# Attention steps that convert expert weights: two experts in each of four early steps, none in the last four

## The chip, the cores and the metric

The kernel runs on one core of a Trainium2 chip. The metric is the device time of one execution in microseconds. Three runs of the kernel before took 386.76, 388.03 and 394.06 us; their median, 388.03 us, is the time before. The profile is of one further execution.

## The reference

Sixteen batch items of 128 rows by 256 columns pass through two stages, each added to its input.

```
x = x + xattn(layernorm(x), ctx)     # per item: theta, phi and g projections to 64 latents, scores, softmax,
                                     # p @ g, normalisation over the whole latent, relu, out projection, + ctx
x = x + moe(layernorm(x))            # 2048 tokens: router softmax, top 2 of 4 groups, top 4 of 16 experts,
                                     # silu(x W1) * (x W3) @ W2 per chosen expert, weighted; plus two shared experts
```

Every product on the expert side is done with 16-bit weights split into a high and a low half. The weights come from memory as 32-bit numbers, 18 sets of them (two shared experts and sixteen routed ones), and have to be converted into the two halves on the chip.

## The kernel before, in words

Attention is a software pipeline over the sixteen items. A step index s runs from 0 to 20; in step s each engine works on parts of several items, and a helper `tile(s, v, lag, part)` (line 326) calls the part for item s minus lag if that item exists. Steps 0 to 7 are written out, steps 8 to 15 are a hardware loop of four steps per pass, steps 16 to 20 are written out again. The order of the calls in each engine's `step` function is the order in which the engine runs them; no engine overtakes within its own list.

The weights ride along in the same steps. SP loads one set (608 KB) at a time into one of two staging buffers, `wst` (line 402); the load for set e waits until set e-2 has been fully converted (line 401, semaphore `wl_ready`). ACT makes the high half with a scaled copy (`weights_high`, line 466, lag 2, the instruction is line 469), which waits for its load; it stands behind `normalise` at the end of the step, and the exponentials of the next step follow it (line 485). DVE makes the low half (`weights_low`, line 1041, lag 3, the instruction is line 1044), which waits for the high half; it stands between the last instruction of the latent normalisation (`latent_out`, line 996) and the second layer norm (`normalise2`, line 1034). So with one set per step ACT converts set s-2 in steps 2 to 19, and DVE set s-3 in steps 3 to 20.

Other lines that the prediction touches: on TensorE the transposes of the softmax p (line 651, they wait for the exponentials), the transposes of the latent (line 676, they wait for DVE's `latent_out`), the product of p and g (`attend`, line 661) and the scores (line 642), in this order around a step's end; the router matmuls (line 698). On DVE the row maximum (line 945) that the exponentials wait for, and the low half of the relu (line 933). On POOL the reciprocal root, an epsilon addition and a power (`rstd`, lines 1440 and 1442), on which `latent_out` and `normalise2` wait; in the later steps POOL also issues the scatters of token rows (line 1460), and `rstd` stands between the second and the third scatter of its step.

After the attention come the units of the shared experts for the first twelve items, with the last four items' routing woven in on DVE, then 80 tiles of the routed experts, then the rest. TensorE waits for all 18 sets only before the routed experts.

Of the kernel before, what the change touches and what calls it, by code (L numbers as in the profile page):

```python
# [35 lines left out]
NU = NE + 2  # L36
# [33 lines left out]
def build(nc, x, ctx_in, params, halves, w_in, out):  # L70
# [4 lines left out]
    with ExitStack() as stack:  # L75
# [152 lines left out]
        def part(n, k):  # L228

            at = 2 * WU + (k * (B // CB) + n) * 2 * CB * T  # L230
            return w[:, at:at + 2 * CB * T].bitcast(F32)
# [94 lines left out]
        def tile(s, v, lag, part, count=B):  # L326

            if not isinstance(s, int) or 0 <= s - lag < count:
                part(s - lag, (v - lag) % 4)

        def group(s, v, lag, part):

            if (v - lag) % 4 == 0 and (not isinstance(s, int) or 0 <= s - lag < B - 4):
                part(s - lag)
# [127 lines left out]
        def _(act):  # L462
# [64 lines left out]
            def step(s, v):  # L527

                tile(s, v, 2, exps)
                tile(s, v, 5, copy_xT)  # L530
                tile(s, v, 1, theta_phi)
                tile(s, v, 2, copy_pT)
                tile(s, v, 3, relu)
                tile(s, v, 4, high)
                tile(s, v, 0, normalise)
                tile(s, v, 2, weights_high, count=NU)
                group(s, v, 8, route_exp)

            def gate(G, n, j, m):
# [20 lines left out]
            def between(stage, n):  # L560
                if stage == "R":
                    route_exp(B - Q)

            pipeline(act, step, units, T_LAG[0], between)

            flat = scatter_rows.rearrange("r c -> (r c)")
# [39 lines left out]
        def _(pe):  # L606
# [108 lines left out]
            def step(s, v):  # L715

                tile(s, v, 2, scores)
                tile(s, v, 4, project_out)
                tile(s, v, 3, mean_all)
                tile(s, v, 1, theta)  # L720
                tile(s, v, 5, transpose_rows)
                tile(s, v, 1, phi)
                group(s, v, 10, count)
                tile(s, v, 2, transpose_p)
                tile(s, v, 1, project_g)
                tile(s, v, 5, router)
                tile(s, v, 3, transpose_h)
                tile(s, v, 2, attend)
# [172 lines left out]
        def _(dve):  # L901
# [106 lines left out]
            def late(s, v, lag, part):  # L1008

                if not isinstance(s, int) or s >= FIRST:  # L1010
                    tile(s, v, lag, part)
# [178 lines left out]
            def step(s, v):  # L1190

                late(s, v, 5, low)
                tile(s, v, 3, attended)
                tile(s, v, 3, latent_stats)
                group(s, v, 10, chosen_diff)
                tile(s, v, 3, latent_aggr)
                group(s, v, 9, route_sum)
                tile(s, v, 3, latent_moments)
                group(s, v, 10, chosen)
                group(s, v, 9, route_recip)  # L1200
                tile(s, v, 2, row_max)
                group(s, v, 10, rank_scan)
                group(s, v, 9, route_score)
                tile(s, v, 4, residual)
                group(s, v, 10, rank_mask)
                group(s, v, 9, group_max)
                tile(s, v, 3, latent_all)
                tile(s, v, 2, values)
                group(s, v, 9, group_compare)
                tile(s, v, 3, latent_var)  # L1210
                tile(s, v, 4, stats2)
                group(s, v, 10, rank_one_hot)
                group(s, v, 10, slots)
                group(s, v, 9, group_equal)
                tile(s, v, 3, latent_centre)
                tile(s, v, 4, aggr2)
                group(s, v, 9, group_before)
                group(s, v, 10, slots_by_rank)
                group(s, v, 9, group_rank)
                tile(s, v, 3, latent_out)  # L1220
                group(s, v, 9, group_choose)
                tile(s, v, 3, weights_low, count=NU)
                group(s, v, 9, mask_mult)
                group(s, v, 10, token_weights)
                group(s, v, 10, destinations)
                group(s, v, 10, slots_sum)
                tile(s, v, 4, normalise2)
                late(s, v, 2, add_context)
                group(s, v, 9, mask_add)
                tile(s, v, 5, logits)  # L1230
                group(s, v, 10, slots_out)
                group(s, v, 9, top_values)
                tile(s, v, 2, recip)
                group(s, v, 9, top_four)
                tile(s, v, 3, relu_low)
                group(s, v, 8, route_max)
                group(s, v, 9, top_replace)
                group(s, v, 8, route_less_max)
# [122 lines left out]
            def last_units(n, first, last):  # L1361
                hidden(SH, n, n % 2, n % 2)
                hidden_low(SH, n, n % 2, SH["hlo_ready"], 1)

            pipeline(dve, step, first_units, D_LAG[0], lambda stage, n: stage in ("A", "R") and between(stage, n))

            def estep(s, step_v, r):
# [195 lines left out]
```

## Time and profile before

| what | value |
|---|---|
| runs, median (lowest to highest) | 388.03 us (386.76 to 394.06) |
| the profiled execution, its own time | 391.98 us |
| its span, first to last instruction | 390.0 us |
| TensorE busy, granted clock over the span | 331.2 us (85%), 0.838 |
| DVE, ACT, POOL busy | 259.5, 221.1, 189.7 us |
| high conversions on ACT, from first to last | 21.7 to 172.0 us |
| low conversions on DVE, from first to last | 27.8 to 173.2 us |

The span is the time between the first and the last instruction of the profiled execution; about 2 us lie around it. A busy share is an average over stages with different limits, so it says little on a change within one stage. The granted clock is the share of TensorE's full rate (2.4 GHz) that it was given: 0.50 is its lower level, 1.2 GHz, and a mean between 0.50 and 1.00 is a mixture of the two. Timelines are in order of start; the number in brackets at the end of a line is how long the engine was idle before it, and on whom it waited.

### The profile page before, as it was taken

What the parts mean: (1) busy time and instruction counts of PE and PEld (TensorE: products, weight loads), DVE (VectorE), ACT (ScalarE), POOL (GpSimd) and SP (SyncE); (2) the same over time, 40 slices, a digit from 0 to 9 for tenths busy, and PEclk for the clock granted to TensorE, in tenths of its full rate; (3) what the DMA queues carried; (4) which work ended last, traced back from release to release, by engine and by line L of the source; (5) the groups of instructions that cost most, each with busy time, mean ns of one, the idle gap of its engine ahead of it and who ended that gap; (6) DMA issues with size and microseconds to landing.
All of it is one profiled execution on the core that took longest, in us unless ns stands there. A gap on an engine that the chain in (4) does not pass through costs nothing.

```text
span 390.0 us, 9314 instructions
## 1 busy us (share of the span) xinstructions
PE 331.2 (85%) x2395; PEld 237.9 (61%) x2396; DVE 259.5 (67%) x982; ACT 221.1 (57%) x553; POOL 189.7 (49%) x223
## 2 busy tenths in 40 slices
PE   0697998877989896337799989999999999997597
PEld 0376666644766674224577757777777777775375
DVE  3457676887788778866845456666566666665774
ACT  0556676755665564245456546666666766663441
POOL 1534333104664665587773006666566656655400
PEclk9998575766565558557999999999999999999699
DMA  8903311222433434353672537797666666779943
GB/s 284 346 1 79 115 64 66 65 66 80 140 124 124 124 126 140 117 165 121 212 263 91 95 70 145 163 155 150 139 154 162 149 142 153 169 209 343 336 154 133
DMA packets 82107, 57.86 MB, mean 148 GB/s; under 512 B 58906, under 2 KB 75549, under 8 KB 82080
## 3 DMA queue, kind: packets, MB, share of 16 engines
q1 hardware_dynamic: 63648, 39.60, 37.7%
q0 software_dynamic: 6912, 17.84, 13.8%
q10 hardware_dynamic: 11520, 0.09, 1.7%
q8 instruction: 13, 0.21, 0.2%
q14 instruction: 14, 0.11, 0.1%
HBM read 24.58 MB, written 24.53 MB: 126 GB/s over the span
## 4 chain that ended last, share of the span: by engine, by line
PE 43%; issue 12%; DVE 11%; POOL 5%; DMA 3%; ACT 2%; POOLq 0%; DVEq 0%; ACTq 0%
PE bank L737 18%; PE bank L755 12%; POOL ranked L1488 4%; DMA ranked<-ctx_all 3%; PE bank L743 2%; PE bank L642 2%; PE bank L883 1%; PE bank L615 1%; PE bank L661 1%; PE bank L745 1%; PE bank L744 1%; DVE w L1044 1%; PE bank L651 1%; PE bank L622 1%; DVE hid L1242 1%
## 5 line engine op out<-in xcount | busy, mean ns | idle before, releaser
L1488 POOL DMA_INDIRECT ranked<-ctx_all x80 | 82.9, 1036 | 75.0 <-ACT ctx_all L588 39.0
L737 PE MATMUL bank<-w,ctx_all 128*128 x480 | 84.7, 312 | 0.4 <-issue 0.4
L755 PE MATMUL bank<-w,hT 128*128 (+3 forms) x560 | 80.6, 275 | 2.8 <-ACT ctx_all L588 2.7
L1460 POOL DMA_INDIRECT slot_rows<-rows_all,slot_k x64 | 65.0, 1015 | 18.0 <-issue 17.4
L737 PEld LDWEIGHTS bank<-w,ctx_all 128*128 128x128 f16 x480 | 46.7, 98 | 19.3 <-issue 0.6
L541 ACT ACTIVATE silu<-bank 128x176 f32<-128x176 f32 x112 | 35.4, 316 | 37.8 <-issue 23.0
L1246 DVE TENSOR_TENSOR hh<-hid,hh 128x48 f16<-128x48 f32 x112 | 23.3, 208 | 50.3 <-ACT hh L546 49.8
L755 PEld LDWEIGHTS bank<-w,hT 128*128 128x128 f16 (+1 forms) x560 | 50.6, 99 | 7.7 <-issue 3.0
L546 ACT ACTIVATE hh<-hid 128x176 f16<-128x176 f32 x112 | 39.0, 348 | 27.8 <-DVE hid L1242 25.2
L1242 DVE SCALAR_TENSOR_TENSOR hid<-bank,silu 128x176 f32<-128x176 f32 x112 | 37.4, 334 | 7.9 <-ACT silu L541 7.5
L588 ACT ACTIVATE ctx_all<-bank,ctx_all 128x256 f32<-128x256 f32 x80 | 37.7, 471 | 7.3 <-DMA ranked<-ctx_all 4.8
L737 PE MATMUL bank<-w,xT_all 128*128 128x352 f16 x192 | 39.0, 348 | 0.0
L1375 DVE COPY hT<-bank 128x384 f16<-128x384 f16 x80 | 28.6, 357 | 13.2 <-PE bank L755 11.0
L743 PE MATMUL bank<-hal,hh 128*128 128x128 f16 x112 | 24.9, 223 | 9.1 <-DVE hh L1247 7.9
L1247 DVE TENSOR_TENSOR hh<-hid,hh 128x128 f16<-128x128 f32 x112 | 32.1, 287 | 0.0
L642 PE MATMUL bank<-ph,th 64*128 64x256 f32 x64 | 27.2, 565 | 0.5 <-ACT ph L477 0.5
L737 PEld LDWEIGHTS bank<-w,xT_all 128*128 128x128 f16 x192 | 20.4, 107 | 10.6
L1044 DVE SCALAR_TENSOR_TENSOR w<-wst,w 128x1216 f16<-128x1216 f32 (+1 forms) x18 | 25.5, 1416 | 0.7 <-ACT w L469 0.7
L485 ACT ACTIVATE p_sb<-bank,nmax 128x256 f32<-128x256 f32 x32 | 14.8, 468 | 19.5 <-DVE nmax L945 19.5
L661 PE MATMUL bank<-g_sb,pT 128*128 128x64 f32 x128 | 24.6, 358 | 0.4 <-ACT pT L493 0.4
L661 PEld LDWEIGHTS bank<-g_sb,pT 128*128 128x128 f32 x128 | 23.5, 275 | 2.4 <-ACT pT L493 2.0
L622 PE MATMUL bank<-ctx_all,par 128*64 128x256 f32 (+1 forms) x32 | 16.5, 616 | 9.8 <-DVE small L929 9.8
(145 smaller groups left out, 565.6 us busy)
## 6 DMA issues: line engine op xcount, KB each, us to landing
wst<-w_dram SPq DMA_DIRECT2D x18, 608.0 KB, 4.0
w<-ranked SPq DMA_DIRECT2D x16, 512.0 KB, 9.3
slot_rows<-pad_rows SPq DMA_DIRECT2D x17, 144.0 KB
x_all<-x_dram SPq DMA_DIRECT2D x4, 512.0 KB, 8.9
ctx_all<-ctx_dram SPq DMA_DIRECT2D x1, 1536.0 KB, 10.6
out_dram<-x_all SPq DMA_DIRECT2D x3, 512.0 KB, 2.9
ctx_all<-slot_rows SPq DMA_TRANSPOSE x80, 3.0
ctx_all<-slot_rows ACTq DMA_DIRECT2D x80, 1.0 KB
```

Source lines behind the costliest of these rows:

```text
L541: A(silu[:, j, :], U[m][:, 0:NF], ACT.Silu, scale=1 / WS).then_inc(G["silu_ready"], 1)
L546: A(hh[:, j, 0:NF], hid[:, j, :], ACT.Copy).then_inc(G["hhi_ready"], 1)
L588: A(y_sb[:, m, :], Y[m % 2][:, 0:T], ACT.Copy, scale=pair(p)[0]).then_inc(EX["y_ready"], 1)
L642: i = mm(SP_[:, h * T:(h + 1) * T], th[:, j, h * P:(h + 1) * P], ph[:, j, :], start=True, stop=True)
L661: i = mm(TS[:, h * L:(h + 1) * L], pT[:, j, k * T + h * P:k * T + h * P + P], g_sb[:, j, k * L:(k + 1) * L], start=k == 0, stop=k == 1)
L737: i = mm(U[j][:, 0:UP1], xt(2 * part + k), up_at(wcol, k, wpart), start=k == 0 and (wpart, part) == (0, 0), stop=k == 1 and wpart == 1)
L743: tr(H16[j][:, 0:P], hh[:, j, 0:FA], ident16)
L755: i = mm(y[:, 0:T], hT[0:rows, j, k * P:(k + 1) * P], down_at(wcol, rows, col), start=start and n == 0, stop=stop and n == len(DOWN) - 1)
L1242: V.scalar_tensor_tensor(hid[:, j, :], U[m][:, NF:UP1], 1 / WS, silu[:, j, :], ALU.mult, ALU.mult).then_inc(G["h_ready"], 1)
L1247: V.tensor_tensor(hh[:, j, NF + FB:2 * NF], hid[:, j, 0:FA], hh[:, j, 0:FA], ALU.subtract).then_inc(done, by)
L1460: G.indirect_dma_start(scatter_rows, bass.IndirectOffsetOnAxis(ap=slot_k[:, b * TOPK + k:b * TOPK + k + 1], axis=0), rows32[:, b * ROW32:( ...
L1488: G.indirect_dma_start(ranked, bass.IndirectOffsetOnAxis(ap=pair(m)[1], axis=0), y_sb[:, m % YR, :], None, bounds_check=(TOPK + 1) * TOKEN ...
```

## The change

A helper `weight_units` takes the place of `tile` for the two conversions. Counted from each engine's own first converting step (step 2 on ACT, step 3 on DVE), the first four steps convert two sets each, 0 to 7, in order; from the fifth on one set per step, set s-lag+4. ACT thus converts sets 0 to 7 in steps 2 to 5 and sets 8 to 17 in steps 6 to 15; DVE does so in steps 3 to 6 and 7 to 16. ACT's steps 16 to 19 and DVE's steps 17 to 20 have no conversion. The number of conversions, the staging buffers, the semaphores and SP's list of loads are as before.

```diff
--- before.py
+++ after.py
@@ -328,6 +328,14 @@
             if not isinstance(s, int) or 0 <= s - lag < count:
                 part(s - lag, (v - lag) % 4)
 
+        def weight_units(s, v, lag, part):
+
+            if isinstance(s, int) and s - lag < 4:
+                for e in range(max(2 * (s - lag), 0), 2 * (s - lag) + 2):
+                    part(e, e % 2)
+            elif not isinstance(s, int) or s - lag + 4 < NU:
+                part(s - lag + 4, (v - lag) % 4)
+
         def group(s, v, lag, part):
 
             if (v - lag) % 4 == 0 and (not isinstance(s, int) or 0 <= s - lag < B - 4):
@@ -533,7 +541,7 @@
                 tile(s, v, 3, relu)
                 tile(s, v, 4, high)
                 tile(s, v, 0, normalise)
-                tile(s, v, 2, weights_high, count=NU)
+                weight_units(s, v, 2, weights_high)
                 group(s, v, 8, route_exp)
 
             def gate(G, n, j, m):
@@ -1219,7 +1227,7 @@
                 group(s, v, 9, group_rank)
                 tile(s, v, 3, latent_out)
                 group(s, v, 9, group_choose)
-                tile(s, v, 3, weights_low, count=NU)
+                weight_units(s, v, 3, weights_low)
                 group(s, v, 9, mask_mult)
                 group(s, v, 10, token_weights)
                 group(s, v, 10, destinations)
```

## Rows read from the trace of the kernel before

**Rows 1.** Windows: steps 4, 5, 6; columns PE, PEld, DVE, ACT, POOL, clock, DMA.

```profile
32.20:40.20 8.00, 5.97 (x34) 4.38 (x32) 5.79 (x18) 5.21 (x12) 2.99 (x5) 0.76 0.28 72
40.20:49.20 9.00, 9.00 (x48) 6.32 (x47) 6.06 (x18) 5.92 (x13) 2.98 (x5) 0.50 0.24 85
49.20:56.90 7.70, 7.70 (x51) 5.08 (x49) 6.14 (x21) 5.85 (x14) 2.97 (x5) 0.72 0.21 72
```

**Rows 2.** Chain of waits, last attention steps; start, length, what ran.

```profile
145.22 1.42 DVE w L1044
...
172.06 1.11 ACT w L469
173.19 1.43 DVE w L1044
```

**Rows 3.** Line view of 1044, all 18 low conversions.

```profile
L1044 DVE SCALAR_TENSOR_TENSOR w<-wst,w x18: 1393/1418/1427, 27.8 to 173.2; 128x1216 f16<-128x1216 f32 x10, 128x1216 f32 x8
```

**Rows 4.** Timeline of SP, the load for expert 2; start, length.

```profile
29.35 0.35 SPq L402 DMA_DIRECT2D wst<-w_dram  x1
```

**Rows 5.** Line view of 402, landing: expert 2's load; then all 18.

```profile
DMA to landing us min/median/max: 3.9/3.9/3.9
...
DMA to landing us min/median/max: 3.6/4.0/9.1
```

**Rows 6.** Timeline of ACT: high conversion, step 3; exponentials, steps 4, 5, 7.

```profile
30.14 1.21 ACT L469 ACTIVATE w<-wst 128x1216 f16<-128x1216 f32 x1
32.24 0.47 ACT L485 ACTIVATE p_sb<-bank,nmax 128x256 f32<-128x256 f32 x1 [0.89 <-DVE nmax L945]
...
40.21 0.47 ACT L485 ACTIVATE p_sb<-bank,nmax 128x256 f32<-128x256 f32 x1 [0.36 <-DVE nmax L945]
...
56.88 0.45 ACT L485 ACTIVATE p_sb<-bank,nmax 128x256 f32<-128x256 f32 x1
```

**Rows 7.** Timeline of DVE: low conversions of steps 3, 4 and 6.

```profile
27.75 1.41 DVE L1044 SCALAR_TENSOR_TENSOR w<-wst,w 128x1216 f16<-128x1216 f32 x1
...
35.58 1.41 DVE L1044 SCALAR_TENSOR_TENSOR w<-wst,w 128x1216 f16<-128x1216 f32 x1
...
52.70 1.41 DVE L1044 SCALAR_TENSOR_TENSOR w<-wst,w 128x1216 f16<-128x1216 f32 x1
```

**Rows 8.** Timeline of PE: steps 4 and 7, transposes of p onward.

```profile
33.31 0.66 PE L651 MATMUL bank<-par,p_sb 128*128 128x128 f32 x4 [0.37 <-ACT p_sb L485]
...
35.80 0.38 PE L676 MATMUL bank<-par,hpre 128*64 128x128 f32 x2 [1.66 <-DVE hpre L996]
36.02 1.43 PE L661 MATMUL bank<-g_sb,pT 128*128 128x64 f32 x8
...
57.94 0.66 PE L651 MATMUL bank<-par,p_sb 128*128 128x128 f32 x4
...
60.51 1.81 PE L661 MATMUL bank<-g_sb,pT 128*128 128x64 f32 x8
```

**Rows 9.** Timeline of DVE: low conversions of steps 17, 18; what follows the first.

```profile
154.24 1.42 DVE L1044 SCALAR_TENSOR_TENSOR w<-wst,w 128x1216 f16<-128x1216 f32 x1
155.58 0.22 DVE L1107 TENSOR_TENSOR masked<-score,gsel 128x64 f32<-128x64 f32 x1
...
164.06 1.42 DVE L1044 SCALAR_TENSOR_TENSOR w<-wst,w 128x1216 f16<-128x1216 f32 x1
```

**Rows 10.** Timeline of POOL, steps 18, 19: power, scatter, epsilon addition.

```profile
162.98 0.72 POOL L1442 TENSOR_TENSOR rs<-veps,par 128x2 f32<-128x2 f32 x1
...
168.13 0.96 POOL L1460 DMA_INDIRECT slot_rows<-rows_all,slot_k  x1 [0.30 <-issue]
169.19 1.30 POOL L1440 TENSOR_SCALAR veps<-mvar 128x1 f32<-128x1 f32 x1
```

**Rows 11.** Line view of 1440, all 17 epsilon additions.

```profile
L1440 POOL TENSOR_SCALAR veps<-mvar x17: 219/232/1302, 26.1 to 169.2; 128x2 f32<-128x2 f32 x15, 128x1 f32<-128x1 f32 x2
```

**Rows 12.** Timeline of PE: the last router matmuls.

```profile
173.87 0.38 PE L698 MATMUL bank<-small,xT_all 128*128 128x16 f16 x8 [0.69 <-ACT xT_all L521]
```

## The prediction

> **What bounds the kernel now.** I read four views, in this order. First the timelines of DVE and ACT, to place the 36 conversions: each costs 1.20 us on ACT [rows 6] and 1.42 us on DVE [rows 3], so the change moves eight of them, four on each engine, and removes none. Whether time is won depends only on which steps have room.
>
> Then the chain of waits, for the steps that lose work. There the reader sees that the last attention steps are not bound by TensorE: the chain runs down DVE's list, with POOL and ACT in between, and three conversions lie on it in person, on DVE at 145.22 and 173.19 and on ACT at 172.06 [rows 2]. After it come the shared units, whose first eight carry the routing of the last items on the same DVE; what the chain gains reaches them.
>
> Then the windows, for the steps that get more work. The chain does not reach back to them. In step 5 TensorE is busy 9.00 of 9.00 us at a granted clock of 0.50, its lower level of 1.2 GHz; in steps 4 and 6 the clock is 0.76 and 0.72 and the step takes 8.00 and 7.70 us [rows 1]. DVE and ACT are busy for 5.2 to 6.1 us of each, so 1.2 and 1.35 us more would fit by their sums. Sums don't decide here, positions do.
>
> Last SP's queue and the landing of its loads, since a conversion can't start before its load, nor the load before the set two places earlier is converted.
>
> **The change part by part, the tail first.** Step 16 loses only an ACT conversion; the exponentials behind it wait for DVE's row maximum, so I put it at nothing. The cover is that wait; without it the price is a gain of up to 1.2 us, which I keep in the bound below.
>
> Step 17: DVE converts at 154.24 and starts the next instruction at 155.58 [rows 9]; DVE's list is the chain here, so 1.34 us come off. Step 18: the same at 164.06 [rows 9], another 1.3 us of DVE's list. Step 19: DVE's conversion is not waited for itself, DVE being idle behind it until POOL has the reciprocal root. But POOL's epsilon addition, which starts at 169.19, takes 1.30 us there [rows 10] where the median of 17 is 0.23 us [rows 11], and it ends as DVE's conversion ends; without the conversion 1.07 us come off. These three would be 3.7 us. They don't all arrive: POOL's addition stands behind a scatter that started 0.30 us after the scatter ahead of it, waiting for nothing else [rows 10], and this run of scatters began behind the power of step 18 at 162.98 [rows 10], which moves only by step 17's 1.34 us, plus some 0.2 us of a gap that closes. So the addition starts 1.5 us earlier and is 1.1 us shorter: 2.6 us. Step 20: ACT's conversion and DVE's behind it end at 174.62 (173.19 plus 1.43) [rows 2], but the router's matmuls of the last item end only at 174.25 [rows 12], and the logits need both; so the 2.5 us of conversions give 0.3 us. **Tail: 2.9 us faster**, between 1.3 us (step 17 alone) and 4.9 us (3.7 without POOL's scatters, and 1.2 of step 16).
>
> **The head.** In step 2 the second conversion falls into ACT's idle time ahead of the exponentials and costs nothing. From step 3 on a new wait appears. Before, a load started in step s is converted in step s+1; now ACT wants it in step s, at the end of the step. DVE's first conversion of step 3 starts at 27.75 and ends at 29.16 [rows 7]; SP issues the load at 29.35 [rows 4]; it lands 3.9 us later [rows 5], at 33.25. ACT is there at 30.14 [rows 6]: 3.1 us of waiting. The second load is issued one DVE conversion later, 1.34 us, lands at 34.6, and its conversion frees ACT at about 35.7 (start to start of ACT's copy is 1.1). From the start of DVE's first conversion to ACT's release that is 1.34 + 1.41 + 0.19 + 3.9 + 1.1, about 8.0 us. Queued behind this wait are the exponentials of step 4, which ran at 32.24 [rows 6]: 3.5 us late. On TensorE the transposes of p then run at 36.8 instead of 33.31; but TensorE had a hole of 1.66 us behind them [rows 8], which is swallowed. The product of p and g needs the transposes (0.66) and ACT's copy of them (0.6): 38.1 against 36.02 [rows 8], **2.1 us late**.
>
> Steps 4 and 5 repeat this. DVE's first conversion of step 4, at 35.58 before [rows 7], comes between 0 and 1.3 us later by the second one of step 3; I take the middle, 0.7, so ACT is free at 44.3, and the exponentials that ran at 40.21 [rows 6] are 4.1 us late. TensorE feels little of that: at the lower clock it works without a hole [rows 1], already 2.1 us behind, and I add 0.6 us: 2.7 us late. That is an estimate between 2.1 and 4.1, nearer the lower end because of the full row of step 5. In step 6 ACT converts one set again, but its load was started by DVE in the same step: 52.70 [rows 7] plus 2.7, plus 1.41 + 0.19 + 4.0 + 1.1, gives 62.1 against 56.88 [rows 6], 5.2 us late, and the exponentials had no slack here (no idle time before them). The transposes of p come at 63.2 instead of 57.94 and the next product at 64.5 instead of 60.51 [rows 8], the hole between them being used up: 4.0 us. From step 7 on a load is again a step ahead of its conversion, and nothing later in attention runs faster than before, so the 4.0 us stay. **Head: 4.0 us slower**, between 2.1 us (TensorE's queue hides all after the first wait) and 5.2 us (nothing of step 6 is swallowed).
>
> POOL in the head: if it is blocked beside DVE's conversion as in step 19 [rows 10, 11], the second conversion of step 3 can hold its subtraction for the normalised input by 1.3 us more, covered by the 3.5 us for which the same step's exponentials are late; without that cover it would cost 1.3 us, so it is inside the bounds. SP's last load waits for set 15, converted in DVE's step 14 instead of 18, so its next write, of padding rows, comes sooner; nobody waits for that. The routed experts wait for all 18 sets long after the last conversion.
>
> **Sum:** 4.0 - 2.9 = 1.1 us slower. Against the profiled execution's own 391.98 us that is 393.1; that execution was 4 us longer than the median of the runs, so on the median it is 388.03 + 1.1 = **389.1 us**. By the bounds: 2.1 - 4.9 = -2.8 and 5.2 - 1.3 = +3.9, 385.2 to 391.9.
>
> **The rivals.** *The waits in the head are swallowed and the tail's gain stays.* For it: TensorE without a hole in step 5 [rows 1], so a late ACT need not be a late TensorE. Against it: the first wait falls into step 3 and 4, where TensorE waited for ACT's exponentials already [rows 8]. It gives 388.03 - 2.9 = 385.1 us.
>
> *The holes cost the clock as well.* TensorE's clock is 0.76 and 0.72 in steps 4 and 6; at 0.50 a step takes 9.00 us [rows 1], so a fall costs 1.0 and 1.3 us: 389.1 + 2.3 = 391.4 us. Against it: step 5 ran at 0.50 with TensorE busy throughout [rows 1], so holes alone do not set the clock. The Trainium skill (TensorE: Matmul & The Clock Gate, Part 1) says that half rate is the default and that activity releases it; by that rule 3 us of new holes in step 4 would speak for this rival, and step 5's row agrees only partly, the clock staying low there under a busy engine.
>
> *The loads come much later when two are in flight.* The first two loads, issued together, took up to 9.1 us [rows 5]. If each of the four waits (steps 3 to 6) grew by 9.1 - 4.0 = 5.1 us, the time would be 389.1 + 20.4 = 409.5 us, well slower. It decides once a pair lands over 2 us later than a single load (8 us over four waits). Against it: those two stood behind the inputs' 4 MB and more, and in steps 4 to 6 the DMA engines are busy for 0.21 to 0.28 of the time [rows 1].
>
> **How the numbers follow.** My forecast 0.55, the swallowed head 0.22, the clock 0.18, the late loads 0.03, something unseen 0.02. The range takes in the bounds and the first two rivals, and a little for the clock falling in one step more: 384.8 to 393.0. What a measurement here can tell from no change is about 2%, 7.8 us; only the late loads pass it, and the spread of the runs before (386.76 to 394.06) leaves a little on both sides: faster 0.03, same 0.91, slower 0.06.
>
> **What would show it.** In the changed profile: ACT idle for about 3 us ahead of its third high conversion, released by the load, and again in steps 4 to 6; the exponentials of step 7 near 62; TensorE's products 4 us late at 64.5 and by the same amount at 140; no conversion on the chain of waits after step 16; POOL's last epsilon addition at 0.23 us; the first shared unit's silu 1 us later than before. I am wrong if ACT's waits are there and TensorE is not late behind step 7, if the tail gives less than 1.3 us, or if a pair of loads lands later than 6 us after its issue.

## The result, and the profile after

The changed kernel takes 395.61 us (median of 4 runs, 394.03 to 396.58) where the kernel before, beside it, took 389.01; the ratio is 1.0182 (95% interval 1.0133 to 1.0231). A second set of runs gave 394.27 against 389.0, ratio 1.0165 (1.0132 to 1.0199). By the ratios, which are not quotients of the medians, that is 6.4 to 7.1 us slower (by the medians 5.3 and 6.6) where I had forecast 1.1, and both times lie above my range (384.8 to 393.0).

The profiled execution took 396.2 us, with a span of 394.3. I read its views in the order of the prediction. The shortest way to the cause is one column of TensorE's timeline: when the product of p and g of an item starts. Its distances from item to item show where time goes, whatever went before:

| us between starts of p·g | 1 to 2 | 2 to 3 | 3 to 4 | 4 to 5 | items 1 to 5 | 5 to 15 | 15 to the table |
|---|---|---|---|---|---|---|---|
| before, profile shown | 7.2 | 8.6 | 9.0 | 6.9 | 31.7 | 94.2 | 37.5 |
| before, second profile | 7.0 | 8.8 | 8.9 | 6.9 | 31.6 | 91.9 | 37.5 |
| after | 11.3 | 9.1 | 11.7 | 9.0 | 41.2 | 91.9 | 34.6 |
| after, second profile | 10.9 | 9.1 | 11.6 | 9.0 | 40.6 | 92.0 | 34.6 |

(Items are counted from 0. The table is the first instruction of DVE that writes the table of the routing, when the shared units are already running.) The head loses 9.0 to 9.5 us, three steps of it; between item 5 and item 15 nothing is lost or given back beyond what two executions of the same kernel differ by; the tail gains 2.9 us. Together +6.1 to +6.6. The distances of one kernel are not quite fixed either: three kernels below, whose first fourteen steps are those of before, take 30.4 to 30.5 us from item 1 to 5, 7.6 of them from item 2 to 3; against those the head's loss is 10.1 to 10.8.

What ACT waits for stands in its timeline (start, length, line, operation; in brackets the idle time before it and who ended it). All times of the page after are 0.4 us later than in [rows 6], because its first exponentials start 0.4 us later.

```profile
33.66 1.22 ACT L477 ACTIVATE w<-wst 128x1216 f16<-128x1216 f32 x1 [3.01 <-DMA wst<-w_dram]
36.53 1.22 ACT L477 ACTIVATE w<-wst 128x1216 f16<-128x1216 f32 x1 [1.66 <-DMA wst<-w_dram]
37.66 0.46 ACT L493 ACTIVATE p_sb<-bank,nmax 128x256 f32<-128x256 f32 x1
...
44.03 1.22 ACT L477 ACTIVATE w<-wst 128x1216 f16<-128x1216 f32 x1 [0.64 <-DMA wst<-w_dram]
45.25 0.47 ACT L493 ACTIVATE p_sb<-bank,nmax 128x256 f32<-128x256 f32 x1
...
54.09 1.22 ACT L477 ACTIVATE w<-wst 128x1216 f16<-128x1216 f32 x1 [0.86 <-DMA wst<-w_dram]
57.31 1.22 ACT L477 ACTIVATE w<-wst 128x1216 f16<-128x1216 f32 x1 [2.00 <-DMA wst<-w_dram]
58.43 0.46 ACT L493 ACTIVATE p_sb<-bank,nmax 128x256 f32<-128x256 f32 x1
```

Five waits for loads, 8.2 us in all, where before there was none. The exponentials behind them start at 37.3, 44.9 and 58.0 (less the 0.4); in the profile before they were at 32.24 and 40.21 [rows 6] and at 49.2. On TensorE the first and the last of these waits stand ahead of the transposes of p of items 2 and 4; before, TensorE waited 0.37 us for the first [rows 8] and not at all for the other (the timeline after, and one line of the same view of before):

```profile
38.71 1.12 PE L659 MATMUL bank<-par,p_sb 128*128 128x128 f32 x4 [4.94 <-ACT p_sb L493]
...
40.52 1.97 PE L669 MATMUL bank<-g_sb,pT 128*128 128x64 f32 x8
47.76 1.12 PE L659 MATMUL bank<-par,p_sb 128*128 128x128 f32 x4
...
59.49 1.12 PE L659 MATMUL bank<-par,p_sb 128*128 128x128 f32 x4 [3.44 <-ACT p_sb L493]
...
61.38 1.87 PE L669 MATMUL bank<-g_sb,pT 128*128 128x64 f32 x8
68.53 1.12 PE L659 MATMUL bank<-par,p_sb 128*128 128x128 f32 x4
```

```profile
51.75 1.12 PE L651 MATMUL bank<-par,p_sb 128*128 128x128 f32 x4
```

So the first and the third late pair reach TensorE, and the second (transposes at 47.76, no wait) is covered by work that was already late. The transposes of item 2 take 1.12 us instead of 0.66. Four windows that follow one another (columns PE, PEld, DVE, ACT, POOL, clock, DMA share, GB/s) answer to [rows 1]; the first two meet where the transposes of item 2 start, the last two run from product to product:

```profile
30.70:39.20 8.50, 3.27 (x17) 2.11 (x18) 6.95 (x19) 3.88 (x8) 2.79 (x6) 0.87 0.52 154
39.20:49.60 10.40, 10.40 (x57) 7.26 (x57) 5.56 (x18) 7.81 (x16) 2.99 (x5) 0.50 0.34 116
49.60:61.40 11.80, 7.58 (x49) 5.16 (x47) 9.55 (x24) 6.91 (x14) 2.97 (x5) 0.64 0.43 133
61.40:70.40 9.00, 9.00 (x47) 6.32 (x47) 5.20 (x16) 5.82 (x13) 2.98 (x5) 0.50 0.27 102
```

The last of them, the step behind the third pair's hole (item 4 to 5), is 9.00 us of a busy TensorE at 0.50, 1.2 GHz. In the profile before, the three windows from product to product, items 2 to 5, are:

```profile
36.02:44.60 8.58, 8.58 (x48) 5.90 (x47) 6.37 (x18) 5.92 (x13) 2.98 (x5) 0.52 0.28 75
44.60:53.58 8.98, 8.98 (x48) 6.30 (x47) 6.03 (x19) 5.92 (x13) 2.97 (x5) 0.50 0.20 69
53.58:60.51 6.93, 5.57 (x49) 4.01 (x47) 5.43 (x19) 5.46 (x13) 2.97 (x5) 0.99 0.26 90
```

So steps that are busy throughout at about 0.50 were there before, from item 2 to 4; what is new is that the step from item 4 to 5, which ran at 0.99, is now one of them.

The landing of the loads, the first of a pair and the second, three pairs (the first two, and the one of step 5), answers to [rows 5]:

```profile
DMA to landing us min/median/max: 3.9/3.9/3.9
DMA to landing us min/median/max: 5.4/5.4/5.4
DMA to landing us min/median/max: 4.0/4.0/4.0
DMA to landing us min/median/max: 4.6/4.6/4.6
DMA to landing us min/median/max: 3.8/3.8/3.8
DMA to landing us min/median/max: 5.6/5.6/5.6
```

In the tail the last DVE conversion starts at 152.61 in the chain of waits, and no ACT conversion stands on it, where [rows 2] has one of each 20 us later; and POOL's epsilon addition never takes its 1.30 us of [rows 10], as its line view shows beside [rows 11]:

```profile
152.61 1.42 DVE w L1052
```

```profile
L1448 POOL TENSOR_SCALAR veps<-mvar x17: 221/238/269, 26.5 to 175.6; 128x2 f32<-128x2 f32 x15, 128x1 f32<-128x1 f32 x2
```

### The profile page after: what moved, and what is told of

It is laid out like the page before. It is cut to its first block, busy times and chain, and to the rows that moved or that the text cites. A ratio compares the mean times of both kernels' runs of the same rounds, so it can differ in the third digit from the quotient of the medians.

```text
span 394.3 us, 9316 instructions
## 1 busy us (share of the span) xinstructions
PE 328.0 (83%) x2395; PEld 236.6 (60%) x2396; DVE 259.5 (66%) x982; ACT 221.2 (56%) x553; POOL 186.9 (47%) x223
## 4 chain that ended last, share of the span: by engine, by line
PE 34%; issue 8%; DVE 7%; POOL 6%; DMA 3%; ACT 1%; POOLq 0%; ACTq 0%; DVEq 0%
PE bank L745 18%; PE bank L763 11%; POOL ranked L1496 4%; DMA ranked<-ctx_all 3%; PE bank L751 1%; PE bank L891 1%; PE bank L752 1%; PE bank L753 1%; POOL slot_rows L1468 1%; DVE hid L1250 1%; POOL rs L1450 1%; DVE x_all L1408 0%; DVE hh L1255 0%; DVE w L1052 0%; DVE repl L1137 0%
## 5 line engine op out<-in xcount | busy, mean ns | idle before, releaser
L1496 POOL DMA_INDIRECT ranked<-ctx_all x80 | 81.3, 1016 | 74.4 <-ACT ctx_all L596 38.2
L1250 DVE SCALAR_TENSOR_TENSOR hid<-bank,silu 128x176 f32<-128x176 f32 x112 | 37.3, 333 | 8.2 <-ACT silu L549 7.9
L596 ACT ACTIVATE ctx_all<-bank,ctx_all 128x256 f32<-128x256 f32 x80 | 37.8, 472 | 6.8 <-DMA ranked<-ctx_all 5.2
L745 PE MATMUL bank<-w,xT_all 128*128 128x352 f16 x192 | 37.9, 341 | 0.0
L751 PE MATMUL bank<-hal,hh 128*128 128x128 f16 x112 | 24.9, 223 | 9.8 <-DVE hh L1255 8.7
L477 ACT ACTIVATE w<-wst 128x1216 f16<-128x1216 f32 (+1 forms) x18 | 21.6, 1206 | 8.2 <-DMA wst<-w_dram 8.2
L659 PE MATMUL bank<-par,p_sb 128*128 128x128 f32 x64 | 17.8, 434 | 9.5 <-ACT p_sb L493 9.5
L753 PE MATMUL bank<-hal,hh 128*128 128x128 f16 x112 | 24.8, 222 | 0.0
L752 PE MATMUL bank<-hal,hh 128*128 128x128 f16 x112 | 24.8, 221 | 0.0
```

The lines of the kernel that those rows point to most:

```text
L596: A(y_sb[:, m, :], Y[m % 2][:, 0:T], ACT.Copy, scale=pair(p)[0]).then_inc(EX["y_ready"], 1)
L745: i = mm(U[j][:, 0:UP1], xt(2 * part + k), up_at(wcol, k, wpart), start=k == 0 and (wpart, part) == (0, 0), stop=k == 1 and wpart == 1)
L751: tr(H16[j][:, 0:P], hh[:, j, 0:FA], ident16)
L752: tr(H16[j][:, P:2 * P], hh[:, j, FA - FZ:NF + FB], ident16)
L753: tr(H16[j][:, 2 * P:3 * P], hh[:, j, NF + FB:2 * NF], ident16).then_inc(done, 1)
L1250: V.scalar_tensor_tensor(hid[:, j, :], U[m][:, NF:UP1], 1 / WS, silu[:, j, :], ALU.mult, ALU.mult).then_inc(G["h_ready"], 1)
```

## The experiments

All ratios are to the kernel before, run on the same chip beside each kernel. "Head" is the distance of p·g from item 1 to item 5 (31.6 before, 41 after), "tail" from item 15 to the table (37.5 before, 34.6 after).

| kernel | median us | before beside it | ratio (95%) | head | tail |
|---|---|---|---|---|---|
| pairs, four staging places | 388.86 | 389.29 | 1.0014 (0.9979 to 1.0049) | 34.6 | 34.6 |
| three pairs, tail as before | 392.97 | 389.29 | 1.0074 (1.0036 to 1.0112) | 35.9 | 37.5 |
| tail alone, sets whole beside units | 388.42 | 389.29 | 0.9994 (0.9957 to 1.0031) | 30.4 | 34.4 |
| first pair loaded early | 392.22 | 389.38 | 1.0073 (1.0036 to 1.011) | 38.2 | 34.6 |
| four places, DVE converts last | 396.45 | 389.38 | 1.0195 (1.0142 to 1.0248) | 37.8 | 34.6 |
| before, DVE converts last | 395.93 | 389.38 | 1.0166 (1.0114 to 1.0219) | 33.6 | 38.8 |
| tail in sixteen quarters | 390.26 | 388.45 | 1.0028 (0.9995 to 1.0062) | 30.5 | 34.5 |
| after, holes filled | 392.64 | 388.45 | 1.0117 (1.007 to 1.0165) | 37.6 | 34.6 |
| tail in fourteen pieces | 388.11 | 388.5 | 1.0009 (0.9971 to 1.0048) | 30.4 | 34.5 |
| before again | 388.79 | 389.0 | 0.9993 (0.9955 to 1.0031) | 31.6 | 37.5 |
| after again | 394.27 | 389.0 | 1.0165 (1.0132 to 1.0199) | 40.6 | 34.6 |

**Pairs with four staging places.** The changed kernel with two more places, in the room of the last two sets' own halves, so that a load is issued two sets earlier.

```diff
         wst = sb("wst", [P, 2, WH])
+        def stage(j):
+            return wst[:, j, :] if j < 2 else w[:, (NU - 4 + j) * WU:(NU - 3 + j) * WU].bitcast(F32)
...
-                wait(sp, S["wl_ready"], e - 1)
+                wait(sp, S["wl_ready"], e - 3 if e < NU - 2 else e - 1)
```

> The changed kernel with four staging places for the loads in place of two (the two more lie where the halves of sets 16 and 17 will be written), so that every load is issued a step ahead of its conversion; the steps in which sets are converted are those of the changed kernel. Theory A, the loss is ACT's waiting for loads at the end of steps 3 to 5: these waits are gone, steps 4 to 7 run as before the change but for 1 to 2 us, the gain of 2.5 us in the last steps stays, and the time is 387 to 390 us, 6 to 8 us under the changed kernel. Rival B, the second conversion itself on ACT and DVE or a lower TensorE clock is what costs: the waits are gone and the time stays at 393 to 396 us.

The waits are gone and with them the loss: 388.86 us. ACT's two conversions now run back to back, without a wait (its timeline, and the windows of the same steps):

```profile
38.97 2.31 ACT L478 ACTIVATE w<-wst 128x1216 f16<-128x1216 f32 x2
...
47.52 2.31 ACT L478 ACTIVATE w<-w 128x1216 f16<-128x1216 f32 x2
```

```profile
44.10:52.70 8.60, 7.56 (x49) 5.07 (x47) 7.10 (x20) 6.69 (x14) 2.97 (x5) 0.70 0.44 145
52.70:61.70 9.00, 9.00 (x47) 6.32 (x47) 7.25 (x20) 5.91 (x13) 2.97 (x5) 0.50 0.43 140
```

Of the head's 9.2 us this takes 6.3; the 2.9 that stay are the price of two conversions in a step even when nothing is late, 2.1 of them in the second window, at the lower clock. That 2.9 and the tail's 2.9 cancel: with the waits gone the change moves work and gains nothing. The 2.9 is one profile's figure; by the ratio's interval (-0.8 to +1.9 us) and the tail's 2.9 it lies between 2.1 and 4.8 us.

**Three pairs, tail as before.** Only sets 0 to 5 in pairs, then two free steps, then one set per step to the end.

```diff
-            if isinstance(s, int) and s - lag < 4:
-                for e in range(max(2 * (s - lag), 0), 2 * (s - lag) + 2):
+            if isinstance(s, int) and s - lag < 3:
+                for e in range(max(2 * (s - lag), 0), min(2 * (s - lag) + 2, 8 - lag)):
                     part(e, e % 2)
-            elif not isinstance(s, int) or s - lag + 4 < NU:
-                part(s - lag + 4, (v - lag) % 4)
+            elif not isinstance(s, int) or 8 - lag <= s - lag < NU:
+                part(s - lag, (v - lag) % 4)
```

> Two staging buffers; pairs only in ACT's steps 2 to 4, none in 5 to 7, and from step 8 on the sets of the kernel before, so the last four steps convert as before the change. Only the waits of steps 3 and 4 are left, and the gain in the last steps is not there. Theory A: the first wait alone makes TensorE some 4 us late and nothing gives it back, so 393 to 394 us (4 to 5 us over before). Rival: most of the loss comes with the second hold in step 5 and the lower clock after it, and the empty steps 5 to 7 give the rest back, so 389 to 391 us.

392.97 us, by the ratio 2.9 slower (by the medians 3.7), just under the 393 to 394 expected if nothing gives the first wait back. The first wait is paid in full (10.9 us from item 1 to 2 instead of 7.1), and the rest of the head runs as before (9.1, 9.0, 6.9). The steps without a conversion gave back at most 1 us: from item 5 to 6 it takes 7.6 us instead of 8.5 or 9.0, and the changed kernel, which converts there, has 7.6 and 8.1. So the first late pair costs 3.9 us by itself, and without the third pair of step 5 and the load of step 6 nothing more is paid in the head. (In this profile the granted clock stands at 1.00 all through items 1 to 5, though the step from item 2 to 3 is 9.13 us of a busy TensorE as after the change, where the clock stands at 0.50: here the column can't be believed, and the lengths decide.)

**The tail alone, and three ways to place it.** The kernel before, with its head untouched; the last four sets are converted beside the shared units, first as whole sets.

```diff
-                tile(s, v, 2, weights_high, count=NU)
+                tile(s, v, 2, weights_high, count=NU - 4)
...
+                if stage == "S" and n in LATE:
+                    weights_high(NU - 4 + LATE.index(n), LATE.index(n))
...
+        LATE = (9, 11, 16, 18)
```

> The kernel before with one set per step to set 13 and sets 14 to 17 converted beside the shared units 9 to 19 instead of in the last four steps; nothing doubled in the head. Theory: this is the tail's gain alone, 2.5 to 2.9 us, so 386 to 387 us. Rival: beside the shared units, where TensorE sets the pace, a conversion of 1.2 us on ACT in a unit of 1.6 us holds TensorE, and the time is 389 us or more.

The tail's 2.9 us appear here as well (34.4), with no pair anywhere, but the time is 388.42, between the two expectations and no gain by the ratio: they are given back beside the units, where TensorE waits for DVE's hh, which it transposes (TensorE's timeline):

```profile
198.13 0.23 PE L748 MATMUL bank<-hal,hh 128*128 128x128 f16 x1 [0.28 <-DVE hh L1252]
200.54 0.23 PE L748 MATMUL bank<-hal,hh 128*128 128x128 f16 x1 [0.63 <-DVE hh L1252]
209.25 0.23 PE L748 MATMUL bank<-hal,hh 128*128 128x128 f16 x1 [0.47 <-DVE hh L1252]
211.31 0.23 PE L748 MATMUL bank<-hal,hh 128*128 128x128 f16 x1 [0.28 <-DVE hh L1252]
214.06 0.23 PE L748 MATMUL bank<-hal,hh 128*128 128x128 f16 x1 [0.96 <-DVE hh L1252]
216.75 0.22 PE L748 MATMUL bank<-hal,hh 128*128 128x128 f16 x1 [0.19 <-DVE hh L1252]
```

Added up 2.81 us, as much as the tail gave. In quarters of 304 columns, one per unit:

```diff
+            def quarter_low(i):
+                e, q = NU - 4 + i // 4, i % 4 * (WH // 4)
...
+                if 0 <= n - 1 - LATE < 16:
+                    quarter_low(n - 1 - LATE)
```

> The kernel before with sets 14 to 17 converted beside the shared units as in the earlier trial, but each cut into four quarters of 304 columns, one quarter per unit on ACT (units 7 to 22) and one unit later on DVE. Theory: the tail's gain is 2.9 us, and the earlier trial gave it back in holes of TensorE beside whole conversions of 1.2 us; quarters fit into the idle time of each unit, the holes shrink under 1 us in all, and the time is 386 to 387.5 us, under both kernels. Rival: the delay per unit adds up whatever the size of the pieces, and the time is 388.5 to 390 us.

390.26 us, at the rival's end. The holes beside the units are gone, but the last quarter comes so late that TensorE waits for it ahead of the routed experts, and the matmuls behind the wait take 1.92 us instead of 1.06:

```profile
218.41 0.22 PE L754 MATMUL bank<-hal,hh 128*128 128x128 f16 x1 [2.06 <-DVE w L1061]
219.52 1.92 PE L748 MATMUL bank<-w,ctx_all 128*128 x6 [0.23 <-issue]
```

In fourteen pieces, to end two units earlier:

```diff
+        LATE_PARTS = [(NU - 4, q, WH // 2) for q in (0, WH // 2)] + [(e, q * (WH // 4), WH // 4) for e in range(NU - 3, NU) for q in range(4)]
```

> Steps 2 to 5 convert one expert each as before the change; experts 14 to 17 are converted beside the shared units instead of beside the last four steps, as in the kernel with sixteen quarters, but in fourteen pieces: expert 14 in halves, 15 to 17 in quarters of 304 columns, so that the last piece falls two units earlier. Theory (the only cost of the sixteen quarters was the last low quarter, for which TensorE waited 2.06 us ahead of the routed experts, and the lower clock behind that wait): the tail keeps its 2.9 us, that wait is gone, and the two halves cost at most the 0.3 to 0.6 us holes that whole conversions made; 385.5 to 387.5 us against 388.5 to 389 of the kernel before, a ratio of 0.992 to 0.997. Rival (a piece that is taken out of the last steps costs TensorE or VectorE as much beside the units, wherever it is put): another wait of 1 to 2 us appears among the units or ahead of the routed experts, and the time stays at 388.5 to 390.5, a ratio of 0.999 to 1.004.

388.11 us, ratio 1.0009: no difference. The 2.06 us wait is gone, yet the stretch from the table to the first routed matmul is 30.5 us long, against 29.5 and 27.9 in the two profiles of before. The windows of that stretch, in the profile shown of before, in its second profile, and here:

```profile
192.22:221.76 29.54, 28.64 (x235) 21.34 (x236) 16.09 (x69) 17.36 (x50) 13.44 (x14) 0.94 0.54 170
```

```profile
190.30:218.20 27.90, 26.97 (x235) 20.60 (x236) 16.07 (x69) 17.38 (x50) 13.51 (x14) 1.00 0.54 172
```

```profile
186.90:217.40 30.50, 28.72 (x235) 21.33 (x236) 21.92 (x84) 21.52 (x64) 14.65 (x15) 0.94 0.65 205
```

The kernel before has this stretch at two clocks: the same 235 matmuls keep TensorE busy for 28.64 us at 0.94 and for 26.97 at 1.00. Against the execution at the same clock, 0.94, the fourteen pieces cost 1.0 us, nearly all of it idle time (1.78 us instead of 0.90). So the ratio came out as the rival said, but of the 2.9 us only this 1.0 is shown to be given back here; whether the pieces also bring the lower clock, one profile can't tell. None of these three beats the kernel before.

**The first pair loaded early.** The changed kernel with the four places, through which all sets go in turn; but only the loads of sets 2 and 3 are issued at the start, and every later load waits, as in the changed kernel, for the set two before it.

```diff
-                wait(sp, S["wl_ready"], e - 1)
+                wait(sp, S["wl_ready"], e - 3 if e < 4 else e - 1)
```

> The changed kernel, but sets 2 and 3 are loaded at the start into two further places, so ACT's wait of step 3 is gone; every later load waits as in the changed kernel for the set two places earlier. Theory A (the wait of a step is paid by TensorE when its queue is empty, and is covered in the step after it): the wait of step 3 moves to step 4, costs some 4 us there, step 5 is covered, and the second payment of the changed kernel in step 5 falls away: 390 to 392 us. Rival B, only the very first wait is paid and all later ones are covered: 387 to 389 us. Rival C, the loss just moves as a whole: 394 to 396 us.

392.22 us, a little above the 390 to 392 expected: by the ratio 2.8 slower than before, under half of the change's loss. The first wait does not go away, it comes one step later and is paid there (ACT's timeline): from item 2 to 3 it takes 11.8 us, while the step from 3 to 4 is back at 9.0. From item 1 to 2, where nothing waits for a load any more, it is still 8.9 instead of 7.1, and from 4 to 5 8.6 instead of 6.9.

```profile
42.47 1.22 ACT L478 ACTIVATE w<-wst 128x1216 f16<-128x1216 f32 x1 [0.68 <-DMA wst<-w_dram]
45.59 1.22 ACT L478 ACTIVATE w<-wst 128x1216 f16<-128x1216 f32 x1 [1.90 <-DMA wst<-w_dram]
```

So two late pairs are paid in full in the changed kernel and one here, though ACT waits for loads in both.

**DVE's conversion at the end of its step.** First in the kernel with four places, to keep it out of the way of the latent normalisation:

```diff
-                weight_units(s, v, 3, weights_low)
...
                 tile(s, v, 3, relu_low)
+                weight_units(s, v, 3, weights_low)
```

> The kernel with four staging places, and DVE's low conversions moved from ahead of the second layer norm to the end of DVE's step, behind the low half of the relu. Theory: with the load waits gone, what the pairs still cost in the head is DVE's pair ahead of the second layer norm, for which ACT waits 1.5 to 2.1 us in steps 4 to 6 in the trace of that kernel; gone, the time is 385 to 387 us, under both kernels. Rival: TensorE's queue covers those waits, or the product behind the pair starts later instead, and the time stays at 388 to 390 us.

396.45 us, 7.6 slower than the same kernel with the old place. My expectation was wrong. The same move in the kernel before, without any pair:

```diff
-                tile(s, v, 3, weights_low, count=NU)
...
                 tile(s, v, 3, relu_low)
+                tile(s, v, 3, weights_low, count=NU)
```

> The kernel before with DVE's low conversions moved to the end of DVE's step, nothing else: a control for the run before it. If the place of a single conversion ahead of the second layer norm matters, 386 to 388 us; if TensorE covers it, no change, 388.5 to 390 us.

395.93 us, outside both expectations: the place alone costs 6.5 us, so the first of the two runs says nothing on pairs. The loss is spread over the attention: 2.0 us from item 1 to 5, 2.2 to 4.6 from item 5 to 15 (96.5 us), 1.3 in the tail. Three lines of this kernel's line view from 15 to 160 us, and the same of the second profile of before (POOL's from 15 to 200; after the bar the sum in us and the mean in ns of one, then the idle time ahead and on whom):

```profile
L1446 POOL TENSOR_TENSOR xn<-xn 128x256 f16<-128x256 f32 x15 | 15.5, 1033 | 18.9 <-ACT xn L517 18.9
L485 ACT ACTIVATE p_sb<-bank,nmax 128x256 f32<-128x256 f32 x32 | 14.9, 470 | 31.5 <-DVE nmax L945 31.5
...
L1450 POOL TENSOR_TENSOR rows_all<-xn,rows_all 128x256 f16<-128x256 f32 x3 | 5.8, 1926 | 5.0 <-ACT rows_all L504 5.0
```

```profile
L1446 POOL TENSOR_TENSOR xn<-xn 128x256 f16<-128x256 f32 x15 | 10.0, 668 | 25.9 <-ACT xn L517 25.9
...
L1450 POOL TENSOR_TENSOR rows_all<-xn,rows_all 128x256 f16<-128x256 f32 x3 | 2.0, 669 | 7.0 <-ACT rows_all L504 7.0
...
L485 ACT ACTIVATE p_sb<-bank,nmax 128x256 f32<-128x256 f32 x32 | 14.9, 469 | 17.6 <-DVE nmax L945 17.6
```

The exponentials wait 31.5 us for DVE's row maximum instead of 17.6, and POOL's two subtractions take 1.03 and 1.93 us on average instead of 0.67. Which of the two carries the 6.5 us was not separated.

**The holes filled.** The changed kernel, with 30 and 20 matmuls whose results are overwritten, ahead of the transposes of p in the two steps with a hole.

```diff
+                wait(pe, S["pt_ready"], b)
+                if isinstance(b, int) and b in (2, 4):
+                    for _ in range(30 if b == 2 else 20):
+                        mm(PT[:, 0:256], ident16, hal[:, 0:256], start=True, stop=True)
                 pe.wait_ge(S["p_ready"], b + 1)
-                wait(pe, S["pt_ready"], b)
```

> The changed kernel with idle matmuls (results overwritten) put on TensorE ahead of the transposes of p in steps 4 (30 of 256 columns) and 6 (20), where it waits 4.9 and 3.4 us for ACT's late exponentials. The waits stay, only TensorE is not idle in them. Theory A, lateness is what costs: no change, 394 to 397 us. Rival, the holes cost the clock: the granted clock of steps 4 and 6 rises from 0.50 and the time falls to 391 to 393 us.

392.64 us, against 395.61 and 394.27 of the changed kernel: 1.6 to 3.0 us of the loss, by time; the intervals of the ratios overlap, so the runs alone would not settle it. The profile does: from item 1 to 5 it takes 37.6 us instead of 40.6 to 41.2, though the waits are all there (12.2 us from item 1 to 2; the first batch of idle matmuls itself ends after the exponentials). The steps behind the holes are the ones that shorten, to 6.9 and 6.8 us from 9.1 and 9.0 (three windows, from about product to product; in the first and the third TensorE is busy for 5.30 and 6.58 us, so the lengths bear out the clock):

```profile
41.00:48.00 7.00, 5.30 (x46) 3.76 (x46) 4.34 (x15) 6.60 (x15) 2.99 (x5) 1.00 0.27 88
48.00:59.70 11.70, 9.64 (x68) 6.32 (x68) 10.10 (x24) 6.79 (x15) 2.96 (x5) 0.85 0.43 124
59.70:66.50 6.80, 6.58 (x44) 4.54 (x45) 4.29 (x15) 5.82 (x14) 2.98 (x5) 0.75 0.43 155
```

**Both kernels once more.** No edit.

> The kernel before, unchanged, in a second profiled execution. Theory (its first profiled execution, 391.98 us, lost some 3 us of TensorE's clock in the attention that most executions don't lose, so the head of the change cost more than a comparison with that trace shows): the ratio is 1.000 within 0.004, and the product of p and g for item 15 starts at 151 to 153.5 us after the start, as in the three kernels whose first fourteen steps are those of before, instead of 154.7; from there to the product's end of the tail (the table) it is 37.5 us again. Rival (the first profile is typical, and the three kernels were quicker because they convert less): item 15's product starts at 154 to 155.5 us.

The theory held: the ratio is 0.9993; items 1 to 5 take 31.6 us as in the first profile, and the product of item 15 starts at 152.8 us instead of 154.7, though item 0 started 0.5 us later. The 2.3 us that the first profile, a longer execution (391.98 us), lost lie after item 5. Read against that profile alone, the changed kernel seems to catch up 2.3 us there, which it does not.

> The changed kernel, unchanged, timed in more runs and in a second profiled execution. Theory (the waits of ACT for the second loads and TensorE's lower clock behind them are the loss, the same in every execution): ratio 1.015 to 1.021, the product of p and g for item 2 at 40 us, for item 4 at 60 to 61 us, for item 15 at 159.5 to 162 us, and 34.6 us from there to the table. Rival (the second wait, in step 5, was an accident of one execution): item 4's product at 57 to 58.5 us, a ratio of 1.008 to 1.012.

Both waits are there again: 10.9 and 11.6 us, and 34.6 us in the tail. The second payment was no accident. Items 2, 4 and 15 come at 38.4, 59.1 and 160.1 us, the first two earlier than I had written, because item 1 was 1.7 us earlier than in the first profile; the distances from item to item agree within 0.5.

## Why the prediction was wrong

**The tail, -2.9 us: right.** It measures 34.6 us instead of 37.5 in both profiles, the same in every kernel without conversions in the last steps (34.4 to 34.6), and 37.5 again in the kernel with three pairs, which keeps them. POOL's addition takes 0.24 us in the median and 0.27 at most, as the working of step 19 had it. Only the sum is shown; the shares of the single steps were not tried apart, and one reading of the working was off: POOL's run of scatters did wait once, 0.53 us for DVE's slots ahead of the scatter at 166.87 in the profile before. That the terms add up to 2.9 may be partly luck.

**The step that failed is the sum of the head: +4.0 us, where 9.0 to 9.5 were measured** (its upper bound was 5.2). The main mechanism was right: ACT idles 3.01 us ahead of its third conversion, against the 3.1 worked out, and with four places, where it doesn't, 6.3 us of the loss are gone. Of its terms the load of a second set and the later start of a pair were too small, the payment of step 5 was missing, and the clock was put at nothing.

- *The second load of a pair.* I let it land 3.9 us after its issue, like the first; it lands 4.6 to 5.6 us after. The exponentials of step 4 therefore start at 37.3 us, not at 35.7, which is 1.5 us of the first payment: that is 3.9 to 4.1 us, not 2.1. The remaining 0.4 or so is the transposes at the lower clock (1.12 instead of 0.66 us).
- *The pair of step 5.* "Steps 4 and 5 repeat this", I wrote, and worked out step 4 and step 6 but never step 5: the full row of [rows 1] let me believe that TensorE would hide it. Step 4 it did hide: from item 2 to 3 it takes 9.1 us instead of 8.6 to 8.8. But DVE then waits for what comes late, 1.42 us for ACT's relu and 1.15 us for TensorE's product; its third pair starts at 48.3 us, where 43.7 us before and the 2.7 us that I allowed it one step later make 46.4, and a second load of 5.6 us follows. The exponentials start at 58.0 instead of 49.2 us, TensorE waits 3.44 us, and the step pays 2.6 to 2.8 us again. A row that is full before the change says nothing on the step once its inputs are late.
- *Step 6.* The 1.3 us that I put there as a wait for a load are 2.1 us of lower clock: 9.0 instead of 6.9 us from item 4 to 5, TensorE busy throughout, no wait ahead of the transposes at 68.53. They stay, as predicted, to the end. With four places this step takes 9.0 us too, so it is not the late loads alone that bring the lower clock.

**The rivals.** The swallowed head (0.22) is out: every payment is in TensorE's timeline. "The holes cost the clock as well" (0.18) was right in kind and nearly in size: I priced it at 2.3 us, and filling the holes brings back 1.6 to 3.0 us by time. I held against it that step 5 runs at 0.50 without a hole; that shows only that holes are not the one cause. The rule that I weighed there, that activity releases the lower clock (the Trainium skill, TensorE: Matmul & The Clock Gate, Part 1), agrees with the run: with idle matmuls in the two holes the steps behind them stand at 1.00 and 0.75 instead of 0.50 and 0.50. The steps that stay at 0.50 for 9 us with TensorE busy throughout, before and after, agree with it no better than step 5's row did. I gave this rival too small a chance. The late loads (0.03) were the right place with the wrong size: it asked for a pair over 2 us later than a single load, and wrong above 6 us; the second load is 0.7 to 1.7 us later, below both marks, and yet this, paid twice on the chain, is over 3 us (1.5 and 1.7 to 1.8). A threshold on a single wait hid that two of them add up.

By these terms: 4.0 forecast for the head, 1.5 and 1.7 us for two second loads, 0.4 for the first transposes and 2.1 less the 1.3 already in it for the clock make 8.4; the last 0.6 to 1.1 us would be the later start of step 5's pair (1.9 us), which was not tried by itself, so that part stays open. The loss of 1.7 to 1.8% stays within 2%, where I had most of the chance, with an interval that reaches 2.3%; the time and its range were wrong.

## What to carry to other kernels

Before work that waits for a transfer is moved a step earlier, write down for each step when its transfer can be issued, including the one behind it in the queue: with two staging places instead of four, a move that gains and loses nothing became a loss of 6 us here. Work out each repetition of a wait by itself, with the inputs late as the one before leaves them; "the rest is hidden" was read from a row that held only without the wait. And before such a change is repaired, price the repaired version: with four places the pairs cost what the tail gains, and none of the three kernels that take conversions to the shared units is faster than before.

## What the runs showed of the hardware

- Two 608 KB loads issued about 1.3 us apart on one queue, after the change: the first lands 3.8 to 4.0 us after its issue, where the loads of before, one per step from 29 to 80 us, take 3.6 to 4.2; the second lands 4.6 to 5.6 us after its own.
- With DVE's conversion at the end of its step, three subtractions of POOL start within 0.01 us of a 1.40 us conversion and take 1.93 us instead of 0.67; its epsilon addition takes 1.30 us beside one [rows 10], instead of 0.23 [rows 11]. The Trainium skill (SBUF — State Buffer, "SBUF: two separate sides") tells of an exclusive lock on a port pair that the two engines share, which blocks the loser for the whole instruction; these rows agree.
- TensorE's clock differs between executions of one kernel: the 235 matmuls between the table and the routed experts keep it busy for 28.64 us in one profile of before, at 0.94, and for 26.97 in the other, at 1.00. From item 5 to item 15 the two take 94.2 and 91.9 us, at 0.61 and 0.68; the two profiles of the changed kernel take 91.9 and 92.0 there at 0.65 and 0.59, so a lower clock is not always a longer stretch. A comparison of single profiles is good to some 2 us here, unless it is made by distances that repeat.
